# A transformer tower kernel: third bf16 part of each projected query/key block formed by GpSimd behind its second part, in place of VectorE

## The reference

```python
h = _L0_tok_ref(0, x, W0, W1, Wo)                  # relu(x W0^T) * (x W1^T), then Wo
h = _layernorm(h + _L0_attn_ref(h, ...))           # 16 heads of 16, window of +-64 tokens
h = _layernorm(h + _L0_ffn_ref(h, ...))            # gate/up/down of 1024, quantised to 8 bits and to ternary weights
h = _layernorm(h + _L1_attn_ref(h, ...))           # 16 heads of 16, causal
h = _layernorm(h + _L1_ffn_ref(h, ...))            # 8 experts of 1024, top 2 with capacity
# attention of either layer:
q, k, v = (split_heads(h @ W + b) for W, b in ((Wq, bq), (Wk, bk), (Wv, bv)))
probs = softmax(q k^T / sqrt(16) + mask)
out = (probs @ v) @ Wo + bo
```

## Time and profile before

| | us |
|---|---|
| median of 3 runs | 963.58 |
| the runs | 954.89 to 964.05 |
| the profiled execution, its own time | 957.48 |
| its span, first to last instruction | 955.7 |

### The profile page before, as it was taken

One profiled execution on the slowest core, in us unless ns is written; L12 is line 12 of the kernel. 1 busy time (PEld: TensorE's weight loads), 2 busy tenths in 40 slices (PEclk: granted clock), 3 DMA queues, 4 the chain that ended last, 5 costly groups with the idle time before them and its releaser, 6 DMA issues. The chain is left out here.

```text
span 955.7 us, 14238 instructions
## 1 busy us (share of the span) xinstructions
PE 838.3 (88%) x4874; PEld 538.1 (56%) x4874; DVE 527.4 (55%) x2057; ACT 442.0 (46%) x793; POOL 309.4 (32%) x389
## 2 busy tenths in 40 slices
PE   6988999998898899999899897289999999999930
PEld 2654465645645545445455344257877877877830
DVE  5267633889879899789777873321311211211236
ACT  1325433588788777787666675123012012012005
POOL 6112422534434433223263525440311311311332
PEclk9997999999999999999899998689999999999975
DMA  9652030222102202202331304431334324322242
GB/s 345 222 205 67 3 89 1 68 68 67 44 26 69 68 1 68 69 2 67 90 95 36 118 24 157 153 84 45 78 83 138 86 75 138 88 72 67 30 113 88
DMA packets 57513, 81.49 MB, mean 85 GB/s; under 512 B 6625, under 2 KB 51042, under 8 KB 55009
## 3 DMA queue, kind: packets, MB, share of 16 engines
q1 hardware_dynamic: 49520, 70.48, 22.9%
q0 software_dynamic: 7296, 9.47, 5.8%
q10 hardware_dynamic: 624, 0.63, 0.2%
HBM read 35.37 MB, written 19.68 MB: 58 GB/s over the span
## 5 line engine op out<-in xcount | busy, mean ns | idle before, releaser
L1134 DVE CUSTOM_DVE_ANT_0 junk<-ps,maskb 128x256 bf16<-128x256 f32 (+4 forms) x512 | 205.1, 435 | 66.4 <-PE ps L845 65.5
L659 ACT ACTIVATE probs<-ps 128x512 f32<-128x512 f32 (+1 forms) x304 | 156.8, 548 | 62.6 <-PE ps L868 61.1
L1585 PE MATMUL ps<-ks,hTe 128*128 128x256 f32 x640 | 143.3, 379 | 0.0
L1608 ACT ACTIVATE hTe<-ps,qs 128x640 f32<-128x640 f32 x64 | 50.8, 794 | 195.9 <-PE ps L1571 195.9
L1571 PE MATMUL ps<-dxT,qs 128*128 128x320 f32 x512 | 140.2, 433 | 0.6 <-DVE dxT L1661 0.5
L1526 POOL DMA_INDIRECT mixed_rows<-ysb,ids x40 | 62.0, 1551 | 223.5 <-DVE ysb L1683 220.5
L1585 PEld LDWEIGHTS ps<-ks,hTe 128*128 128x128 f32 x640 | 119.3, 190 | 15.1
L1571 PEld LDWEIGHTS ps<-dxT,qs 128*128 128x128 f32 x512 | 96.7, 190 | 40.1 <-DVE dxT L1661 0.8
L868 PE MATMUL ps<-qs,ks 99*128 99x256 bf16 (+4 forms) x512 | 103.0, 286 | 15.3 <-DMA qs<-nrows 6.6
L845 PE MATMUL ps<-ks,qs 96*128 96x256 bf16 (+4 forms) x512 | 105.4, 289 | 3.9 <-DVE nmax L1134 1.5
L884 PE MATMUL ps<-probs,vaug 128*32 128x256 f32 (+4 forms) x1024 | 87.4, 414 | 7.5 <-POOL probs L556 4.4
(11 more groups left out here) (197 smaller groups left out, 1219.6 us busy)
## 6 DMA issues: line engine op xcount, KB each, us to landing
qs<-parts SPq DMA_DIRECT2D x96, 128.0 KB, 2.4
ks<-parts SPq DMA_DIRECT2D x96, 128.0 KB, 2.4
qs<-w SPq DMA_DIRECT2D x8, 1024.0 KB, 9.6
ks<-w SPq DMA_DIRECT2D x8, 1024.0 KB, 5.0
dispatched_rows<-att SPq DMA_DIRECT2D x8, 650.0 KB, 10.6
ks<-dispatched_rows SPq DMA_DIRECT2D x4, 650.0 KB, 7.4
x_sb<-xT SPq DMA_DIRECT2D x8, 256.0 KB, 3.9
mixed_rows<-h SPq DMA_DIRECT2D x4, 512.0 KB, 3.1
```

What stands on the lines that cost most here:

```text
L659: act.activation(probs_of(u)[:, heads[0]:heads[-1] + 1, :], turned_bank((u, half, i))[:, 0:len(heads) * w].rearrange("p (j n) -> p j n", n=w),
L1134: ins = dve.tensor_tensor_reduce(out=junk[:, b - (b > V_BANK), a * (hi - lo):(a + 1) * (hi - lo)], in0=score_bank((u, half, i))[:, a * (hi ...
L1585: ins = mm(bank(4 + n % 2)[:, 0:D], hTe[:, e % 2, m, t * P:(t + 1) * P], w2s[:, e % 2, m, :], start=(m == 0), stop=(m == MH - 1))
L1608: act.activation(hTe[:, e % 2, m, :].rearrange("p (a n) -> p a n", a=2), ps[:, 2 * (n % 2):2 * (n % 2) + 2, 0:HC], ACT.Silu, bias=b1s[:, e ...
```

## The change

GpSimd forms part 2 of each of the 32 blocks right behind part 1, in the same step, after a wait on its own semaphore. VectorE no longer forms it. ScalarE's and SyncE's waits on `part2_done` stay as they are. VectorE also gets one wait for its own mask conversion, once, at half -4.

```diff
@@ GpSimd, dense
                             pool.wait_ge(rest_done, n + 1)
                             pool.tensor_copy(parts[:, c - 2, 1, :], proj[:, c % 2, :]).then_inc(part1_done, 1)
+                            pool.wait_ge(part1_done, n + 1)
+                            pool.tensor_tensor(parts[:, c - 2, 2, :], proj[:, c % 2, :], parts[:, c - 2, 1, :],
+                                               ALU.subtract).then_inc(part2_done, 1)
@@ VectorE, dense
                         if phase == "qkv":
-                            j = c - 3
-                            if 0 <= j < 2 * NB:
-                                dve.wait_ge(part1_done, 2 * NB * i + j + 1)
-                                dve.tensor_tensor(parts[:, j, 2, :], proj[:, j % 2, :], parts[:, j, 1, :],
-                                                  ALU.subtract).then_inc(part2_done, 1)
                             j = c - 2
@@ VectorE, half -4
                             dve.tensor_copy(maskb[:, :], mask_in).then_inc(mask_done, 1)
+                            dve.wait_ge(mask_done, 1)
```

## The result

The changed kernel takes 953.02 us (median of 10 runs, 950.82 to 954.02), the kernel before 960.62 over the runs beside it: the ratio is 0.9923 with a 95% interval of [0.9895, 0.9951]. That is 7.4 us less, where I forecast 5.0 (the ratio is taken of means and leaves out one run of the kernel before, of 2611 us; the medians differ by 7.6 us with that run and by 6.7 without it). The interval reaches from 4.7 to 10.1 us. The profiled execution took 953.76 us, its span 951.7 at a mean granted clock of 0.944 (before: 957.48, 955.7, 0.948).

The account below looks back on a forecast made before the run. From 200 to 470 us TensorE leads, idle 26.09 us, with VectorE close behind at 86%. Savings of 4.24 + 1.54 less 0.8 given back make 5.0 us, off the 963.58 median: 958.5 us, range 950 to 966.

Parts of the forecast that it names:

- ScalarE's wait: Phases 3 to 5: ScalarE's copy no longer waits for VectorE's late part 2; TensorE saves 1.64, 1.64 and 0.96 us.
- VectorE itself: Phases 3 and 4: removed subtractions shorten TensorE's gaps ended by VectorE, 0.77 us a phase, 1.54 us; bounds 0 and 2.2.
- Given back: Of the 5.8 us saved, 0.8 us is lost at later waits.
- GpSimd's cost: 32 subtractions of 1.27 us on GpSimd, 40.6 us in all, cost 0 on the path; 5.1 us if unhidden in phase 7.
- the lead of 4.3 us: Phase 7: GpSimd's select ends 4.3 us before its values product begins, enough to hide two added subtractions' 2.5 us delay.
- The late case: Phase 7: GpSimd, behind indirect DMAs, delivers part 2 half a microsecond late for ScalarE; taken as 0, bound 0.6 us.
- The collisions: GpSimd's new subtractions can hold up VectorE operations, at most 0.5 us of VectorE a block.
- The signs named beforehand: Checks in waits, gaps and durations; GpSimd waits in phase 7 or 1, or far larger shortening in phases 3 to 6, refute.
- TensorE's three gaps behind line 745: Gaps of 0.70, 0.94 and 0.96 us in phases 3 to 5, forecast to disappear.
- The gaps move: Rival, phases 3 and 4: shortening one wait lengthens the next; 0 to 1.5 us remain, 963 us; chance 0.24.
- VectorE is the real bound: Rival, 200 to 470 us: about 12 us of VectorE's removed time come back, 951.6 us; chance 0.13.
- GpSimd late: Rival, phases 7, 0 and 1: GpSimd's slower subtraction lengthens steps, up to 9.8 us, 973.4 us; chance 0.11.

Follow-up runs that it names:

- run 2: Kernel before, part 2 still on VectorE; from phase 3 on blocks 2 and 3 keep their rests in `x_sb`, so ScalarE's wait goes: 956.83 us, ratio 0.9973.
- run 9: Changed kernel, but GpSimd forms part 2 in phases 0, 1, 2, 6 and 7 alone, VectorE in 3 to 5: 959.27 us, ratio 0.9997.
- run 10: Changed kernel, but phase 7's part 2 left to VectorE: 952.48 us, ratio 0.9915.
- run 8: Changed kernel, but GpSimd forms part 2 in phases 3 to 5 alone, VectorE as before elsewhere: 951.46 us, ratio 0.9913.
- run 6: Kernel before, part 2 still on VectorE but formed one half earlier from phase 2 on: 955.88 us, ratio 0.9936.
- run 11: As run 8, with part 2 formed one half earlier on VectorE in phases 2, 6 and 7: 949.50 us, ratio 0.9887.
- run 5: Changed kernel plus an unused one-input reduction on VectorE, 20 times from phase 3 on: 958.35 us, ratio 0.9990.
- run 3: Changed kernel plus an unused subtraction of two SBUF inputs on VectorE, 20 times from phase 3 on: 963.31 us, ratio 1.0038.
- run 7: Changed kernel plus a second, unused subtraction on GpSimd, 20 times from phase 3 on: 957.17 us, ratio 0.9987.

## Why the prediction was right

**ScalarE's wait: right in place and size.** Forecast 4.24 us. Run 2 isolates it: phase 3 at clock 0.97, 64.62 to 62.73, 1.89 us; phase 4 at 1.00, 63.84 (run 9) to 62.27, 1.57; phase 5 at 1.00, 69.77 to 68.60, 1.17. Together 4.6.

**VectorE itself: the term that was mis-sized.** I took 0.77 us in each of phases 3 and 4, 1.54 in all, with 2.2 as the upper bound. Run 10 against the kernel before gives the whole gain at equal clocks: 3.38, 3.44 and 1.08 us, 7.9 in all; run 8 (with run 9 beside it in phase 5) gives 3.21, 3.08 and 1.24, 7.5 in all. Less ScalarE's 4.6 that leaves 2.9 to 3.3, above my bound, and all of it in phases 3 and 4: phase 5 gives 1.1 to 1.2 us with VectorE's relief or without it. The step that failed was reading VectorE's share from the two gaps that named it in the trace of before. With ScalarE's gaps away, three VectorE gaps of 0.79, 0.58 and 0.78 us stand in phase 3 (run 2), 2.15 us where the trace of before names VectorE for 0.43 + 0.92: ScalarE's late copies had covered the rest. The two waits ended close together, and only a kernel with one of them gone shows the other. That is not the whole of it. TensorE's idle time in the three stretches (length less busy time) falls from 20.0 us before to 14.2 in run 10, by 5.85 us, which is what I had added up from gaps (5.8). The other 2.05 of the 7.9 us are busy time of the same matmuls, 180.4 against 178.3 us, which no gap shows; why it is shorter stays open.

**Given back: nothing, not 0.8.** In run 10 the values product of half 163 starts 7.97 us earlier than before (counted from the first of them), and the last one of all 7.98: the later stages keep the gain. Where the changed kernel's profile seems to lose (15.57 to 17.91 us for the last of the halves) its clock was 0.81 against 0.99. Run 9, without the gain, has 17.89 us at 0.81 there too.

**GpSimd's cost: right.** 1211 ns on average, at best 1154, against the 1.27 taken from line 589. The values products wait hardly longer for it: the idle time that GpSimd's selects released is 19.8 us in all, 19.1 before, and the lead of 4.3 us is still 3.1. The late case in phase 7 cost TensorE one gap of 0.39 us, within its bound of 0.6.

**The collisions: allowed for, and there.** 0.5 us a block was the allowance, 16 us in all; VectorE's busy time fell by 10.5 us less than was removed from it, 5.5 of it in the four operations of `split_maxima`. Those follow GpSimd's subtractions: they lose 1.7 us with the twelve of run 8 and 3.9 with the twenty of run 9. The rests did not become faster (772 to 778 ns), against my forecast of some 680: the new subtraction seems to meet some of them. They fall only where part 2 comes one half earlier on VectorE, to 715 ns in run 6 and 735 in run 11; with GpSimd in three phases alone (run 8) they are at 766. The Trainium skill, "SBUF — State Buffer", section "Who interferes with whom", says of this chip that a reduction never contends with GpSimd; by that rule run 5 put its load back without collisions of its own, and the trace agrees: 661 to 681 ns in all 20, where the subtraction of run 3 reached 1118.

**The signs named beforehand.** TensorE's three gaps behind line 745 are gone, and the new line is near 1.27 us. Three signs did not come as written: the rests are no nearer to 0.68 us, 1.3 us of "issue" are left, and line 747 waits for GpSimd, in phases 0 and 7. The last is one of the two signs by which I would have called the prediction wrong, in phase 7; it cost TensorE 0.39 us. The other, a stretch that shortens by much more than the named gaps, came half true: 7.9 us where 5.8 were named. So the mechanism held, with VectorE's part too small and GpSimd's lateness in phase 7 larger than nothing.

**The rivals.** "The gaps move" is out for phases 3 and 4: gaps did come behind VectorE, but the change relieved it too. In phase 5 it has a share of the truth, with 1.13 us behind VectorE in place of 0.96 behind ScalarE, though the phase is 1.1 us shorter all the same. "VectorE is the real bound" had a share of the truth, in phases 3 and 4 only: 12 us were not there, and run 9 shows that its time is worth nothing elsewhere. "GpSimd late" has its point of decision between the 1.2 us a block of the change and the 2.6 of run 7.

**The level.** 958.5 was 5.5 us above the 953.0 measured. Of these, 3.0 are the median of three runs on which I built (963.58 against 960.62 over ten), the rest the saving. Both errors go the same way; it was the width of the range that took them. The time of the whole kernel would not have shown that a term was mis-sized, since 5.0 us lies inside the interval of 4.7 to 10.1: only the stretches at equal clock do.

## What to carry to other kernels

When two engines release a third close together, the trace names only the later one; the earlier one's price shows when the first is gone, so put a wider bound on the engine that is 86% busy beside it. A queue's order can cost nearly as much as its load: one half earlier on the same engine won 5.5 us by the medians, where the change won 7.6. Move work only in the stages where the wait is (12 of 32 moves gave all of it), and double the moved work once to see how much room is left.

## What the runs showed of the hardware

**The time follows the granted clock.** The kernel before, in one batch of 31 runs: median 963.9 us at a mean clock of 0.943 (10 runs), 961.4 at 0.945 (9), 957.5 at 0.948 (3), 952.4 at 0.953 (4). That is 11.5 us for 0.01 of clock, more than the change's gain, so small ratios must be read beside the clock. The order does not hold for every pair: run 7 took 956.1 us at 0.946 (4 runs) and 958.0 at 0.948 (1 run). Run 2 shows what that does to a verdict: at 0.945 it took 956.8 us (5 runs) and the kernel before 961.7 (8 runs), 4.9 less, where the medians of all runs say 2.5. Inside an execution the clock is at one of two levels, 1.2 or 2.4 GHz (0.50 in three windows of 2 us from 572 to 578 us of the changed kernel, 1.00 from 580 on). Phase 3 took 61.24 us at a mean of 0.97 (run 10) and 62.84 at 0.95 (the changed kernel) with the same instructions.

**A 16-column operation can cost as much as a 512-column one.** Beside a GpSimd subtraction of 1.17 us, a VectorE subtraction of 16 columns took 0.88 us against a mean of 218 ns before, and ended with it. The conversion of 16 columns that started 0.02 us ahead of it took its usual 0.20 us, so in this case what was under way was not held up. Conversions can be hit too: line 1158, with a median of 199 ns, took 1091 ns once.
